# Every signal of TensorE given by a drain behind the last matmul of its group

## The reference: two graph layers on eight graphs of 2048 nodes

```python
# layer 0
idx = the first 25 neighbours of each node (top_k of -column where adj != 0)
agg = max over these 25 rows of x                      # max(agg, 0) where degree <= 25
x   = layernorm(x + relu(concat([x, agg]) @ W0 + b0))
# layer 1, 4 heads of 64
h      = x @ W[head]
weight = leaky_relu(e_src[i] + e_dst[j]) where adj, else -1e9
att    = softmax(weight)                               # over j, 2048 wide
dst    = att @ h + bias
out    = relu(dst) + h, normalised over each head's 64, times gamma plus beta
x      = layernorm(x + out)
```

## Time and profile before

| | |
|---|---|
| median of 3 timed runs | 5439.7 us (5429.06 to 5457.46) |
| span of the profiled execution | 5448.3 us |
| granted TensorE clock, mean (1 is 2.4 GHz, 0.5 is 1.2 GHz) | 0.778 |
| busy: PE, DVE, ACT, POOL | 63%, 76%, 57%, 68% |
| chain that ended last: POOL, issue, DVE, PE | 36%, 25%, 22%, 8% |

### The profile page before, as it was taken

One profiled execution on the slowest core, in us unless ns is written; L12 is line 12 of the kernel. 1 busy time (PEld: TensorE's weight loads), 2 busy tenths in 40 slices (PEclk: granted clock), 3 DMA queues, 4 the chain that ended last, 5 costly groups with the idle time before them and its releaser, 6 DMA issues.

```text
span 5448.3 us, 58256 instructions
## 1 busy us (share of the span) xinstructions
PE 3438.2 (63%) x11778; PEld 1438.1 (26%) x11778; DVE 4138.1 (76%) x11484; ACT 3111.4 (57%) x5570; POOL 3717.1 (68%) x3204
## 2 busy tenths in 40 slices
PE   1232467666666767666676666666666666666786
PEld 1121222222222222222222222222222222222222
DVE  4555578878787888878787878888878788787777
ACT  3333456666556666656655655656656666555565
POOL 4666777777777777777777777777777777677400
PEclk9555578777778777878777787787888778778798
DMA  3434344444444444444444444444444444444210
GB/s 113 130 119 136 119 138 128 146 132 146 125 129 133 135 144 135 132 143 129 134 133 133 145 125 127 139 130 146 136 144 131 128 139 131 137 131 133 85 39 27
DMA packets 282021, 692.71 MB, mean 127 GB/s; under 512 B 62849, under 2 KB 130178, under 8 KB 265346
## 3 DMA queue, kind: packets, MB, share of 16 engines
q0 software_dynamic: 153600, 419.64, 26.1%
q1 hardware_dynamic: 128130, 270.41, 15.6%
HBM read 639.21 MB, written 50.59 MB: 127 GB/s over the span
## 4 chain that ended last, share of the span: by engine, by line
POOL 36%; issue 25%; DVE 22%; PE 8%; DMA 4%; ACT 3%; another core or an unknown queue 1%; POOLq 0%; DVEq 0%; SPq 0%; ACTq 0%
POOL rows L498 36%; PE acc L1231 5%; DVE uv L819 5%; DVE rmax L836 4%; DMA rows<-in_x_dram,idx 4%; DVE top L715 2%; DVE key_b L717 1%; PE pB L1199 1%; DVE agg L845 1%; DVE sth L892 1%; ACT uv L565 1%; DVE key_a L717 1%; DVE mvh L898 1%; ACT stage L525 0%
## 5 line engine op out<-in xcount | busy, mean ns | idle before, releaser
L498 POOL DMA_INDIRECT rows<-in_x_dram,idx x3200 | 3716.9, 1162 | 1404.5 <-issue 997.0
L1231 PE MATMUL acc<-uv,hs 128*65 128x512 f32 x4096 | 2301.4, 712 | 707.2 <-DVE uv L819 448.3
L565 ACT ACTIVATE uv<-rb,qj 128x512 f32 (+1 forms) x2048 | 1330.4, 712 | 169.6 <-PE acc L1231 137.6
L819 DVE SCALAR_TENSOR_TENSOR uv<-uv,maskT 128x1024 f32<-128x1024 f32 x1024 | 1239.9, 1221 | 183.6 <-ACT uv L565 148.4
L1231 PEld LDWEIGHTS acc<-uv,hs 128*65 128x65 f32 x4096 | 602.6, 160 | 1992.7 <-issue 1403.4
L836 DVE TENSOR_TENSOR rmax<-rmax,rows 128x1280 f32<-128x1280 f32 x384 | 572.5, 1491 | 600.4 <-DMA rows<-in_x_dram,idx 553.5
L628 ACT ACTIVATE xaT<-pA 128x512 f32<-128x512 f32 x128 | 76.4, 597 | 791.3 <-PE pA L1186 610.6
L542 ACT ACTIVATE stage<-pT 128x1024 bf16<-128x1024 f16 x256 | 260.6, 1018 | 288.8 <-remote 148.0
L1186 PE MATMUL pA<-id,xt 128*128 128x128 f32 x256 | 81.5, 419 | 469.4 <-DVE agg L846 334.2
L640 ACT ACTIVATE x1T<-pA 128x256 f32<-128x256 f32 x128 | 49.2, 384 | 570.8 <-PE pA L1209 394.5
L1199 PE MATMUL pB<-w_sb,xaT 128*128 128x256 f32 x1024 | 348.0, 499 | 18.4 <-ACT xaT L628 8.6
(11 more groups left out here) (113 smaller groups left out, 3755.5 us busy)
## 6 DMA issues: line engine op xcount, KB each, us to landing
adj_sb<-in_adj_dram SPq DMA_DIRECT2D x128, 1024.0 KB
rows<-in_x_dram,idx POOLq DMA_INDIRECT x3200
xh_dram<-xh SPq DMA_DIRECT2D x128, 256.0 KB
rb<-r_dram SPq DMA_DIRECT2D x32, 1024.0 KB
xr<-xh_dram SPq DMA_DIRECT2D x64, 512.0 KB
xt<-in_x_dram SPq DMA_DIRECT2D x128, 128.0 KB
out_dram<-xr SPq DMA_DIRECT2D x32, 512.0 KB
r_dram<-er SPq DMA_DIRECT2D x128, 2.0 KB
```

Source lines behind the costliest of these rows:

```text
L498: nc.gpsimd.indirect_dma_start(rows[:, c, r * C:(r + 1) * C], None, x_rows, bass.IndirectOffsetOnAxis(ap=idx[p][:, k:k + 1], axis=0)).then ...
L565: last = nc.scalar.activation(uv[k][:, i, :], rb[:, bass.ds(qa % 2, 1), h, :].rearrange("p a i -> p (a i)"), ACT.Copy, scale=q_j(h))
L819: nc.vector.scalar_tensor_tensor(uv[k][:], uv[k][:], 1.0, m, ALU.max, ALU.mult).then_inc(s_u, 1)
L1231: last = nc.tensor.matmul(acc[h][0:HW, :], hs[:, (1 - quad.par) * JT + jt, h, :], uv[k][:, i, :], start=(jt == 0), stop=(jt == JT - 1))
```

## The change

Each group of matmuls or transposes of the main program now gives its signal by a drain instruction that stands behind its last matmul, where before the last matmul gave it. The matmuls, their order, every wait and all other engines are as they were, apart from line numbers (L1209 becomes L1210, L1215 becomes L1216, L1217 becomes L1218, L1231 becomes L1232). `pe.drain()` is an instruction of PE's queue that is done when the matmuls ahead of it are.

```diff
--- before.py
+++ after.py
@@ -1143,8 +1143,8 @@
                         pe.wait_ge(s_ring, v)
                     for j in range(HALF):
                         jt = hf * HALF + j
-                        last = nc.tensor.transpose(pT[hf][:, j * P:(j + 1) * P], mask_sb[:, jt * P:(jt + 1) * P], id16[:])
-                    last.then_inc(s_T, 1)
+                        nc.tensor.transpose(pT[hf][:, j * P:(j + 1) * P], mask_sb[:, jt * P:(jt + 1) * P], id16[:])
+                    pe.drain().then_inc(s_T, 1)
 
             def pack_words(quad, u, g_of):
 
@@ -1157,8 +1157,8 @@
                 for v in quad.reach(lambda q: QT * q + u + g_of - 2):
                     pe.wait_ge(s_proj, v)
                 for jt in range(JT):
-                    last = nc.tensor.matmul(p_key[:, jt * WPT:(jt + 1) * WPT], stage[:, jt, :], pack[:], start=True, stop=True)
-                last.then_inc(s_key, 1)
+                    nc.tensor.matmul(p_key[:, jt * WPT:(jt + 1) * WPT], stage[:, jt, :], pack[:], start=True, stop=True)
+                pe.drain().then_inc(s_key, 1)
 
             def back(quad):
 
@@ -1167,8 +1167,8 @@
                     pe.wait_ge(s_sT, v)
                 for i in range(QT):
                     for h in range(HEADS):
-                        last = nc.tensor.transpose(acc[i][:, h * HW:(h + 1) * HW], sT[:, h, i * P:(i + 1) * P], id32[0:HW, 0:HW])
-                last.then_inc(s_back, 1)
+                        nc.tensor.transpose(acc[i][:, h * HW:(h + 1) * HW], sT[:, h, i * P:(i + 1) * P], id32[0:HW, 0:HW])
+                pe.drain().then_inc(s_back, 1)
 
             def transpose_xa(quad, u):
 
@@ -1183,8 +1183,8 @@
                     pe.wait_ge(s_proj, v)
                 for c in range(4):
                     src = (xt[p] if c < 2 else agg)[:, c % 2 * P:(c % 2 + 1) * P]
-                    last = nc.tensor.transpose(pA[:, c * P:(c + 1) * P], src, id32[:])
-                last.then_inc(s_xaT, 1)
+                    nc.tensor.transpose(pA[:, c * P:(c + 1) * P], src, id32[:])
+                pe.drain().then_inc(s_xaT, 1)
 
             def product0(quad, u):
 
@@ -1197,7 +1197,8 @@
                     pe.wait_ge(s_xaE, v)
                 for c in range(4):
                     nc.tensor.matmul(p_lin, xaT[:, c, :], w0_sb[:, c, :], start=(c == 0), stop=False)
-                nc.tensor.matmul(p_lin, ones_row[:], b0_sb[:], start=False, stop=True).then_inc(s_lin, 1)
+                nc.tensor.matmul(p_lin, ones_row[:], b0_sb[:], start=False, stop=True)
+                pe.drain().then_inc(s_lin, 1)
 
             def product1(quad, u):
 
@@ -1206,16 +1207,16 @@
                 for v in quad.reach(lambda q: QT * q + u):
                     pe.wait_ge(s_x1, v)
                 for c in range(2):
-                    last = nc.tensor.transpose(p_x1T[:, c * P:(c + 1) * P], xh[p][:, 0, c * P:(c + 1) * P], id32[:])
-                last.then_inc(s_x1T, 1)
+                    nc.tensor.transpose(p_x1T[:, c * P:(c + 1) * P], xh[p][:, 0, c * P:(c + 1) * P], id32[:])
+                pe.drain().then_inc(s_x1T, 1)
 
                 for v in quad.reach(lambda q: QT * q + u):
                     pe.wait_ge(s_x1E, v)
                 for c in range(2):
                     nc.tensor.matmul(p_h, x1T[:, c, :], wcat[:, c, :], start=(c == 0), stop=(c == 1))
                 for c in range(2):
-                    last = nc.tensor.matmul(p_es, wcat[:, c, C:C + HEADS], x1T[:, c, :], start=(c == 0), stop=(c == 1))
-                last.then_inc(s_h, 1)
+                    nc.tensor.matmul(p_es, wcat[:, c, C:C + HEADS], x1T[:, c, :], start=(c == 0), stop=(c == 1))
+                pe.drain().then_inc(s_h, 1)
 
             def attend(quad, u, a, b):
 
@@ -1228,9 +1229,9 @@
                         pe.wait_ge(s_u, v)
                     for i in range(2):
                         h = 2 * hh + i
-                        last = nc.tensor.matmul(acc[h][0:HW, :], hs[:, (1 - quad.par) * JT + jt, h, :], uv[k][:, i, :],
+                        nc.tensor.matmul(acc[h][0:HW, :], hs[:, (1 - quad.par) * JT + jt, h, :], uv[k][:, i, :],
                                                 start=(jt == 0), stop=(jt == JT - 1))
-                    last.then_inc(s_pe, 1)
+                    pe.drain().then_inc(s_pe, 1)
 
             def step(quad, u):
                 if u == 0 and quad.on(u, FIN):
```

## The result

The changed kernel took 5600.2 us (median of 4 runs, 5565.1 to 5621.1), the kernel before beside it 5448.6 us (5429.1 to 5465.4): a ratio of 1.0286 [1.0232, 1.0341]. Measured twice more, it gave 1.0204 [1.0169, 1.0240] and 1.0155 [1.0125, 1.0186]. The forecast was 80 us more, the three answers are 152, 119 and 77 us. Ratios leave out executions that stood apart as slow (among them one of `double`, at 6291.9 us, whose cause no trace shows).

What follows compares the result with a forecast made beforehand. No engine was full: a ring of POOL's gathers and DVE bounded most steps, PE the last 327 us. Terms of 32, 40 and 8 us added 80 to the span, 5528, or 5520 us as timed median; range 5455 to 5610.

Steps and rivals of the forecast that it cites:

- One drain: On PE in a burst: 0.21 us of lost overlap plus 0.17 us of reaction, 0.38 us.
- 210 groups: Drained groups counted on the recorded chain over the whole span, at 0.38 us each: 80 us.
- The further 0.138 us: Per drain on PE, the weight load's lost cover: 0.52 us a drain, 109 us in all.
- Last part: From 5121 us on, no gathers, PE the bound: 84 groups on the chain cost 32 us.
- the hand-overs: Some 90 last groups of chain pieces, handing over to another engine, pay less than 0.38 us; taken as offset.
- First steps: Steps before 651 us: 22 groups on the chain at 0.38 us, 8 us.
- the steps with gather and attention: From 651 to 5121 us: 104 groups on the chain at 0.38 us, 40 us.
- paths that now lie just under the chain come up: Near-critical paths would add time; taken as equal to what cheaper hand-overs save, so nothing net.
- A: Rival: DVE's wait for gathered rows, 5.7 us a step, absorbs the drains; 0 to 27 us, chance 0.16.
- D: Rival: ten drains in a row lengthen the start of all 28 blocks; 106 us instead of 40, 5586, chance 0.17.
- B: Rival: PE's clock stays low, PE bounds the gather steps too; near 6055 us, partial fall 5620 to 5800, chance 0.09.
- C: Rival: the drain answers when matmuls are handed over, so hand-overs come 0.2 us sooner; 5422 us, chance 0.03.

Runs made afterwards that it cites:

- double: Changed kernel with a second, bare drain ahead of each drain that signals; 1.0142 of the kernel before.
- tail_only: Kernel before with drains only in the 16 steps without a gather; 1.0031 [0.9989, 1.0073], inconclusive by its ratio.
- units_only: Kernel before with drains only behind the 1024 units of attention; 1.0195 of the kernel before.
- groups_only: Kernel before with drains only behind the 928 groups that are not units of attention; 1.0058 of the kernel before.
- both edits: 1 MB adjacency load held until DVE takes the third chunk, and unit 6 moved behind idx at u = 0; 0.9842 without drains, 0.9905 with all drains.
- start_only: Kernel before with drains only behind ten groups in a row at each block's start, 320 of 1952; 5448.8 us, 1.0068.
- before_u6: Kernel before, no drains, with unit 6 moved behind idx at u = 0; 5346.7 us, 1.0011.
- after_third: The changed kernel itself, measured a third time against the kernel before; 5425.3 us, 1.0155.

## Why the prediction was wrong

The direction was right, and the time lies in the range (5600 against 5455 to 5610), near its end. An excess of 80 us was forecast; the first comparison gave 152.

- **One drain, 0.21 + 0.17 = 0.38 us.** Measured 0.42. By 210 groups that is 88 us, not 80. Both parts hold: the lost overlap is 0.21 (1.93 - 1.72), the idle time behind the drain 0.21 where I took 0.17. The Trainium skill's page "TensorE: Matmul & The Clock Gate" (the table at its head, Engine queue depth) has weight loads pulled ahead of matmuls in flight. The further 0.138 us, by which the prediction weighed the loss of that, is not there: four passes and the gap are 1.93 + 0.21 = 2.14.
- **Last part, 84 x 0.38 = 32 us.** Measured 27 (25 to 29 over the three runs). In a session of their own tail_only and units_only take 20 and 21 us more here, and groups_only nothing. That the 84 paid less than 0.38 us each fits the hand-overs that I had named and not weighed; no run separates them.
- **First steps, 22 x 0.38 = 8 us.** Measured 4, -5 and, at the quicker level, 4 us (604.2 for 599.9): at most half, and not to be told from nothing, as this part took 654 to 669 us at the slower level whatever the kernel. PE is busy for only 189 us of these 655.
- **The failed step: the steps with gather and attention, 104 x 0.38 = 40 us.** Measured 106 and 87 us where I had the profile, 53 at the quicker level. The term counted groups on the one chain that the trace gave and priced them alike. It was mis-sized, and not by the price of a drain: 104 x 0.42 = 44 us. What I set at nothing net was the sentence "paths that now lie just under the chain come up. I leave them equal". The runs name two such paths: unit 6 at u = 0, and the landing of the third chunk with the load behind it. With the other one out of the way, either carries 47 to 48 us of the middle, and only with both out of the way is the delay gone. In the first run unit 6's wait grew by 42 us, and 11 more late chunks of some 3.5 us make 39: 81 of the 106 us, if they simply add, which no run shows. In the second the two give 31 + 32 of 87. The rest, with the late drains as a candidate, stays open. So does how much of the count of 104 is owed to a trace that lacked part of its releases.
- **A (the gather's cushion takes it)** is right for the middle of one pair of kernels: with both edits it hides every drain. In the given kernel it did not hold, though DVE's wait for rows, 5.7 us a step, is fifteen times one drain: unit 6 stands behind that wait, with no other wait between it and idx that would take its loss up, and the late chunk lengthens the wait itself.
- **D (all blocks' starts, 106 us)** came nearest by its sum, which is luck: start_only costs 36 us. Its kind of cause, near-critical paths in all blocks, is what happened, and one of the two places, unit 6 at u = 0, is at a block's start (59 us of wait in start_only, for 31); the other is not.
- **B (the clock falls)** is wrong: 0.778 became 0.797. **C** is wrong: units moved apart by 0.42 us.
- **What the profile was to show.** Units 2.1 us apart: yes. The clock within 0.03: yes. The last stretch +30: 27. PE's busy time near 3438: no, 3553; each record's fill counts again when nothing lies beside it. Idle before L1232 that nothing releases +400: 141.5 us at the quicker level, 642 times, since half of a drain's price appears as busy time and a unit whose uv came late shows DVE as its releaser. POOL's wait for idx +40: all of POOL's idle time before its gathers grew by 127 us in the first comparison, three times my number and the plainest sign of the mis-sized term. At the quicker level, where all releases are recorded, that wait is 421.7 us in the third run against 383.6 in before_u6, 38 more.

```profile
POOL rows L498 <- DVE idx L768: 421.7, 121, 43.2
...
PE acc L1232 <- issue: 141.5, 642, 0.4
```

## What to carry to other kernels

A drain behind a group costs its overlap with the next group plus the restart, here 0.42 us, and it costs that even where its signal is nobody's; here the signal on the last matmul was the cheaper way in every pair. Delays off the chain were not free in this ring of engines: count the places just below the chain and the transfers whose start they shift, and give the sum of the chain's terms as a lower end. To find such places, take them out one by one and together; here one edit alone left most of the cost in the other place. Where a change moves a large load against small gathers, look for a landing with two typical values and hold the load: that was worth 46 us here, where the change cost 77 to 152. And before comparing the wait rows of two traces, compare how many waits of a kind that must occur once per tile they hold.

## What the runs showed of the hardware that was not expected

- A 1 MB load issued before the last small indirect gather of a chunk has ended makes the chunk ready 5.2 to 5.5 us after the gather (medians of the profiles), where it is 1.87 us when the load is issued later. In each profile 1 to 8 steps lie between, most of them with the load within 0.3 us of the gather's end. With the load held, none of the steps of four profiles is over 4 us.
- A second drain directly behind the first costs 0.08 us, a first 0.42.
- At the quicker level the drain's signal is only 20 ns later than a matmul's own (35 against 15 ns after the modelled end). At the slower level some are late by far more: at `back` up to 7.29 us in the first run and 7.49 in the second.
- The granted clock rose with drains behind all groups in every pair of profiles (0.778 became 0.797; 0.783 became 0.798 with unit 6 moved; 0.791 became 0.805 with the load held; 0.789 became 0.804 with both). One of the six executions of `after_third` had 0.729, at 5456.7 us for a median of 5425.3; it has no trace.
- The same kernel ran at 5345 or at 5413 to 5480 us in different sessions, and the traces of the slower level hold about half of the semaphore events of the quicker. The steps before attention show the level best (600 to 609 us to the first unit, or 654 to 669).
